# Second cross-attention: scores from the normalized tokens times one product of Wq and K per batch, layer norm's scale and bias on the tokens

## The reference

```python
xn = _layer_norm(_layernorm(x), ln_scale, ln_bias)       # normalized twice, then scale and bias
q = (xn @ Wq).reshape(B, T, 8, 64).transpose(0, 2, 1, 3) * 64 ** -0.5      # Wq: 256 x 512
k, v = jnp.split(y @ Wkv, 2, axis=-1)                    # y: the context, 77 rows a batch; 8 heads of 64
sim = jnp.einsum('bhid,bhjd->bhij', q, k)                # 1024 x 77 a head
attn = softmax(sim)
out = jnp.einsum('bhij,bhjd->bhid', attn, v) @ Wo
x = x + tanh(g_xattn[1]) * out
```

## Time and profile before

| | |
|---|---|
| device time, median of 3 runs | 1934.1 us (1932.99 to 1936.02) |
| the profiled execution | 1928.68 us, its span 1926.9 us |
| granted TensorE clock over the span | 0.987 |
| TensorE busy over the span | 1822.4 us (95%) |
| VectorE, ScalarE, GpSimd busy | 1169.6, 1066.1, 732.6 us |
| second cross-attention | about 917 to 1142 us |

### The profile page before, as it was taken

One profiled execution on the slowest core, in us unless ns is written; L12 is line 12 of the kernel. 1 busy time (PEld: TensorE's weight loads), 2 busy tenths in 40 slices (PEclk: granted clock), 3 DMA queues, 4 the chain that ended last, 5 costly groups with the idle time before them and its releaser, 6 DMA issues.

```text
span 1926.9 us, 59938 instructions
## 1 busy us (share of the span) xinstructions
PE 1822.4 (95%) x26285; PEld 1488.6 (77%) x26285; DVE 1169.6 (61%) x1646; ACT 1066.1 (55%) x1883; POOL 732.6 (38%) x1008
## 2 busy tenths in 40 slices
PE   6999799999999999999899988999999999999996
PEld 4666578888877888888799877888788777888775
DVE  7888533332423333232555549888888888888785
ACT  5666444443434344343344546777677677777663
POOL 6999500000010000000233333564656565655542
PEclk9999999999999999999899999999999999999999
DMA  5332100000000000010211024212432142224210
GB/s 163 106 112 70 50 1 22 1 23 1 22 7 17 22 1 23 0 68 6 75 41 46 24 93 106 75 56 61 118 85 65 56 124 81 63 62 119 58 53 31
DMA packets 147003, 106.21 MB, mean 55 GB/s; under 512 B 19992, under 2 KB 143152, under 8 KB 146736
## 3 DMA queue, kind: packets, MB, share of 16 engines
q1 hardware_dynamic: 146736, 102.28, 18.0%
HBM read 76.77 MB, written 25.49 MB: 53 GB/s over the span
## 4 chain that ended last, share of the span: by engine, by line
PE 40%; ACT 6%; issue 3%; DVE 2%; POOL 0%; DMA 0%; POOLq 0%; DVEq 0%; ACTq 0%
PE E_ps_o L2009 12%; PE E_ps_s L1990 5%; PE E_ps_o L1954 5%; PE C_ps_y L1086 3%; PE E_ps_o L1971 3%; PE C_ps_m L1047 2%; PE E_ps_o L1961 2%; PE C_ps_s L1062 2%; ACT head L2197 2%; ACT e_raw L2208 1%; ACT E_prob L2171 1%; PE C_ps_t L1073 1%; DVE E_negmax L2487 1%; ACT e_raw L2254 1%; PE E_ps_o L2030 1%
## 5 line engine op out<-in xcount | busy, mean ns | idle before, releaser
L2171 ACT ACTIVATE E_prob<-E_ps_s,E_negmax 128x1024 f32<-128x1024 f32 x256 | 284.9, 1116 | 145.2 <-DVE E_negmax L2487 144.8
L2487 DVE TENSOR_REDUCE E_negmax<-E_ps_s 128x1 f32<-128x1024 f32 x256 | 301.5, 1220 | 87.6 <-PE E_ps_s L1990 87.3
L2494 DVE STREAM_TRANSPOSE E_prob<-E_prob 128x1024 f32<-128x1024 f32 x256 | 303.9, 1225 | 23.9 <-ACT E_prob L2171 11.4
L2009 PEld LDWEIGHTS E_ps_o<-E_prob,E_vrep 32*64 32x64 f32 x15872 | 232.3, 130 | 71.2 <-ACT head L2197 55.8
L2009 PE MATMUL E_ps_o<-E_prob,E_vrep 32*64 32x128 f32 x15872 | 265.0, 274 | 17.9 <-issue 8.4
L1588 ACT ACTIVATE F_raw<-F_ps,ffn_scales 128x512 f32<-128x512 f32 x128 | 88.4, 690 | 287.9 <-PE F_ps L1490 287.9
L1490 PE MATMUL F_ps<-F_ha,ffn_w_rounded 128*128 128x512 f32 x1024 | 240.7, 396 | 0.0
L1490 PE MATMUL F_ps<-F_hb,ffn_w_rounded 128*128 128x512 f32 x1024 | 240.2, 395 | 0.0
L1490 PEld LDWEIGHTS F_ps<-F_ha,ffn_w_rounded 128*128 128x128 f32 x1024 | 191.2, 188 | 48.1 <-issue 1.7
L1490 PEld LDWEIGHTS F_ps<-F_hb,ffn_w_rounded 128*128 128x128 f32 x1024 | 192.4, 188 | 46.5
L2390 POOL TENSOR_TENSOR head<-head 128x512 f32<-128x512 f32 x93 | 119.2, 1281 | 256.3 <-ACT head L2197 256.3
(11 more groups left out here) (306 smaller groups left out, 3761.8 us busy)
## 6 DMA issues: line engine op xcount, KB each, us to landing
E_vrep<-E_v_all SPq DMA_DIRECT2D x128, 256.0 KB, 3.1
shared<-in_L_ffn_h_wT SPq DMA_DIRECT2D x16, 512.0 KB, 3.9
E_v_all<-E_vst SPq DMA_DIRECT2D x32, 256.0 KB, 2.2
C_x<-x SPq DMA_DIRECT2D x20, 256.0 KB, 4.2
F_x<-x SPq DMA_DIRECT2D x9, 512.0 KB, 3.8
A_x<-in_x SPq DMA_DIRECT2D x16, 256.0 KB, 5.1
x<-A_x SPq DMA_DIRECT2D x16, 256.0 KB, 2.2
x<-F_x SPq DMA_DIRECT2D x16, 256.0 KB, 2.1
```

What stands on the lines that cost most here:

```text
L2009: mm = pe.matmul(low[64 * j:64 * j + 64, g, :], vrep[rows, slot, KB // 4 * (quarter % 2) + k, dh * j:dh * (j + 1)], prob[rows, u % 2, :, j ...
L2171: act.activation(prob[:, s // UT % 2, s % UT, j, :], ps_s[:, j, :], ACT.Exp, bias=negmax[:, at:at + 1], scale=1.0, accum_out=den[:, 2 * c ...
L2487: dve.tensor_reduce(negmax[:, at:at + 1], ps_s[:, j, :], AX.X, ALU.max, negate=True).then_inc(d_max, 1)
L2494: dve.transpose(at, at).then_inc(d_t, 1)
```

## The change

The q projection goes. Once per batch, K of every head is multiplied by the transposed Wq of that head (`qk_proj`, two chunks k of the model dimension), which gives a matrix `qk` of 256 x 616, kept as hi and lo fp32r tiles: ScalarE writes hi with the softmax scale, VectorE lo. The scores of a tile are the transposed tokens (stationary, hi and lo) times `qk` (moving, 308 columns for 4 heads). Norm's scale and bias are put on the tokens when they leave PSUM: ScalarE's copy becomes two activations with scale and bias, VectorE's `x_low` first computes the same in fp32 (`xf`) and then subtracts. `qbias`, `wq_hi`, `wq_lo`, `q` and the 16 one-column instructions go. K's and V's projections stand in one step (8b - 7), `qk_proj` in the next two (8b - 6, 8b - 5), `u_proj` in two groups (four blocks, one block) at 8b - 4 and 8b - 3; `ps_u` has two banks for one, `ps_m` one for two. Wq is laid out transposed on the way in.

```diff
-        K_AT, V_AT, U_AT = {-7: 0}, {-6: 0}, {-2: (0, 0), -1: (0, 1), 0: (0, 2)}
+        KV_AT, M_AT, U_AT = {-7: 0}, {-6: (0, 0), -5: (0, 1)}, {-2: (0, 0), -1: (0, 1)}
...
-            K_AT[8 * b - 7], V_AT[8 * b - 6] = b, b
-            U_AT.update({8 * b - 5 + i: (b, i) for i in range(3)})
-        U_BLOCKS = ((0, 1), (2, 3), (4,))
+            KV_AT[8 * b - 7] = b
+            M_AT.update({8 * b - 6 + i: (b, i) for i in range(2)})
+            U_AT.update({8 * b - 4 + i: (b, i) for i in range(2)})
+        U_BLOCKS = ((0, 1, 2, 3), (4,))
...
+            def kv_proj(b):
...
+                for i, (w, made) in enumerate(((wk, e_k), (wv, e_v))):
+                    for c in range(C):
+                        for k in range(DC):
+                            mm = pe.matmul(ps_u[:, i, c * S:(c + 1) * S], w[:, k, c * P:(c + 1) * P],
+                                           cx[:, b % 2, k, :], start=k == 0, stop=k == DC - 1)
+                    mm.then_inc(made, 1)
+
+            def qk_proj(b, k):
+                pe.wait_ge(k_made, b + 1)
+                pe.wait_ge(v_made, b + 1)
+                if k:
+                    pe.wait_ge(m_out, 2 * b + 1)
                 for c in range(C):
...
+                    for g in range(RG):
+                        rows = slice(RT * g, RT * (g + 1))
+                        mm = pe.matmul(ps_u[:, g, c * S:(c + 1) * S], wqT_sb[rows, c, k * P:(k + 1) * P], kt[rows, c, :],
+                                       start=True, stop=True)
+                mm.then_inc(e_m, 1)
...
-            def q_proj(n):
-
-                pe.wait_ge(x_out_of, n + 1)
...
             def scores(T):
                 n, t = divmod(T, 2)
                 b = n // PB
-                pe.wait_ge(q_made, n + 1)
+                pe.wait_ge(x_out_of, n + 1)
                 if T % (2 * PB) == 0:
-                    pe.wait_ge(k_made, b + 1)
+                    pe.wait_ge(m_out, 2 * b + 2)
                 if T:
                     pe.wait_ge(d_sub, T)
-                for c in range(C):
-                    for g in range(RG):
-                        rows = slice(RT * g, RT * (g + 1))
-                        mm = pe.matmul(ps_s[:, g, c * HR * S:(c + 1) * HR * S], q[rows, n % 2, c, t * TOK:(t + 1) * TOK],
-                                       kt[rows, b % 2, c, :, :], start=True, stop=True)
+                for g in range(G):
+                    ops = [(k, a, m) for k in range(DC) for a, m in split_passes(xt, qk)]
+                    for i, (k, a, m) in enumerate(ops):
+                        mm = pe.matmul(ps_s[:, g, 0:4 * S], a[:, n % 2, k, t * TOK:(t + 1) * TOK],
+                                       m[:, b % 2, k, 4 * S * g:4 * S * (g + 1)], start=i == 0, stop=i == len(ops) - 1)
                 mm.then_inc(e_s, 1)
...
-                act.activation(xt[0][:, n % 2, :, :], ps_m[:, 0, :].rearrange("p (c w) -> p c w", c=DC),
-                               ACT.Copy).then_inc(x_hi, 1)
...
+                for k in range(DC):
+                    ins = act.activation(xt[0][:, n % 2, k, :], ps_m[:, k * PAIR:(k + 1) * PAIR], ACT.Identity,
+                                         bias=ln_sb[:, 1, k:k + 1], scale=ln_sb[:, 0, k:k + 1])
+                ins.then_inc(x_hi, 1)
...
+            def qk_evacuate(b, k):
+                act.wait_ge(e_m, 2 * b + k + 1)
                 if b >= 2:
                     act.wait_ge(e_s, 2 * PB * (b - 1))
...
+                act.activation(qk[0][:, b % 2, k, :].rearrange("p (c g s) -> p g c s", g=RG, s=S),
+                               ps_u[:, :, 0:C * S].rearrange("p g (c s) -> p g c s", s=S),
+                               ACT.Copy, scale=SCALE).then_inc(m_hi, 1)
...
             def x_low(n):
                 dve.wait_ge(x_hi, n + 1)
...
+                for k in range(DC):
+                    own.link(dve.tensor_scalar(xf[:, k, :], ps_m[:, k * PAIR:(k + 1) * PAIR], ln_sb[:, 0, k:k + 1],
+                                               ln_sb[:, 1, k:k + 1], ALU.mult, ALU.add))
+                own.wait()
+                dve.tensor_tensor(xt[1][:, n % 2, :, :], xf[:, :, :], xt[0][:, n % 2, :, :],
+                                  ALU.subtract).then_inc(x_out_of, 1)
+
+            def qk_low(b, k):
+                dve.wait_ge(m_hi, 2 * b + k + 1)
+                for g in range(RG):
+                    hi, lo = (m[:, b % 2, k, :].rearrange("p (c g s) -> p g c s", g=RG, s=S)[:, g, :, :] for m in qk)
+                    ins = dve.scalar_tensor_tensor(out=lo, in0=ps_u[:, g, 0:C * S].rearrange("p (c s) -> p c s", s=S),
+                                                   scalar=SCALE, in1=hi, op0=ALU.mult, op1=ALU.subtract)
+                ins.then_inc(m_out, 1)
```

More of the change, by code:

```diff
@@ L874, in cross_attention @@
     B, _, S = ctxT.shape
-    HD = wqT.shape[1]
+    HD = wkT.shape[1]
     dh = HD // H
@@ L907, in sb @@
             return ctx.enter_context(nc.sbuf_tensor(f"{tag}_{name}", shape, dt))
-        qbias = sb("qbias", [P, C])
-        kt = sb("kt", [P, 2, C, HR, S])
+        kt = sb("kt", [P, C, S])
+        qk = [sb("qk_hi", [P, 2, DC, H * S], F32R), sb("qk_lo", [P, 2, DC, H * S], F32R)]
         vt = sb("vt", [P, (C + 1) * (TWO + P)])
@@ L1033, in x_transpose @@
                         each = head[:, 2 * n + t, :] if n < HEAD else xn[:, n % 2, t, :]
-                        mm = pe.transpose(ps_m[:, 0, at:at + TOK], each[:, c * P:(c + 1) * P], ident[:, :])
+                        mm = pe.transpose(ps_m[:, at:at + TOK], each[:, c * P:(c + 1) * P], ident[:, :])
                 mm.then_inc(e_x, 1)
-            def q_proj(n):
-                pe.wait_ge(x_out_of, n + 1)
[L1040 to L1049, removed]
             def scores(T):
@@ L1090, in _ @@
             x_transpose(0)
[L1091 to L1096, removed]
             for T in STEPS:
@@ L1102, in _ @@
                     p_transpose(T, 0)
[L1103 to L1107, removed]
+                if not odd and 0 < n + 2 < NP:
+                    x_transpose(n + 2)
                 if 0 <= T < TILES:
@@ L1111, in _ @@
                     out(T - 1)
[L1112 to L1115, removed]
+                if T in KV_AT:
+                    kv_proj(KV_AT[T])
+                if T in M_AT:
+                    qk_proj(*M_AT[T])
                 if T in U_AT:
@@ L1184, in _ @@
             act.activation(warm[:, :], warm[:, :], ACT.Exp)
[L1185 to L1188, removed]
             for T in STEPS:
@@ L1192, in _ @@
                     prob_out(T, 0)
-                if 0 <= n + 2 < NP:
-                    if odd:
-                        q_evacuate(n + 2)
-                    elif n + 2:
-                        x_evacuate(n + 2)
+                if not odd and 0 < n + 2 < NP:
+                    x_evacuate(n + 2)
                 if 0 <= T < TILES:
@@ L1340, in _ @@
                     x_low(0)
-                    for k in range(DC):
-                        ins = dve.tensor_scalar(wq[0][:, k, :], wq_raw[:, k, :], ln_sb[:, 0, k:k + 1], None, ALU.mult)
-                    ins.then_inc(wq_hi, 1)
-                    dve.wait_ge(wq_hi, 1)
-                    for k in range(DC):
-                        ins = dve.scalar_tensor_tensor(out=wq[1][:, k, :], in0=wq_raw[:, k, :],
-                                                       scalar=ln_sb[:, 0, k:k + 1], in1=wq[0][:, k, :],
-                                                       op0=ALU.mult, op1=ALU.subtract)
-                    ins.then_inc(wq_lo, 1)
                 b, p = divmod(T + 12, 8)
@@ L2640, in gated_layers @@
         c_ln = ctx.enter_context(nc.sbuf_tensor("c_ln", [P, 2, DC], F32))
-        HD, rows = t["L1_xattn_Wq"].shape[1], "(c p) n -> p c n"
-        c_wq, c_wk, c_wv = (shared[:, i, :].rearrange("p (c n) -> p c n", n=HD) for i in range(3))
-        c_wo = shared[:, 3, :].rearrange("p (c n) -> p c n", n=D)
+        HD, rows = t["L1_xattn_Wk"].shape[1], "(c p) n -> p c n"
+        c_wk, c_wv = (shared[:, i, :].rearrange("p (c n) -> p c n", n=HD) for i in (1, 2))
+        c_wq, c_wo = (shared[:, i, :].rearrange("p (c n) -> p c n", n=D) for i in (0, 3))
         early = ((c_wq, t["L1_xattn_Wq"].rearrange(rows, p=P)),
```

75 lines of the change are left out of this document (32 added, 43 removed).

## The result

The changed kernel took 1914.8 us (median of four runs, 1912.1 to 1917.7), the kernel before 1933.9 beside it: a ratio of 0.990, 95% interval 0.988 to 0.992, 19 us less. Forecast were 12.5 us less and a time of 1915.5 to 1929.0. The profiled execution took 1917.1 us, its span 1914.7: 12.2 us less than the span before.

The account below looks back on a forecast made before the run. TensorE's queue was taken to bound the second cross-attention. Terms -40.3 + 18.5 + 6.3 + 0.5 + 2.2 = -12.8 us, called -12.5, taken off the 1934.1 median gave 1921.6 us; range 1915.5 to 1929.

Parts of the forecast that it names:

- Bound: Second cross-attention, after the first few tiles: the stage lasts as long as TensorE's queue, busy 189.1 of 190 us.
- B: Rival: VectorE's loop takes over in the second cross-attention, giving 11 us back; total -1.5, 1932.6 us; chance 0.09.
- Term (1): TensorE behind the scores of tile 3: pairs 2 to 15 lose their q projection, 14 x 2.88 = -40.3 us.
- Term (2): Scores on TensorE: twelve 308-column fp32r instructions at 143 ns, 1.71 us a tile, +0.66; +18.5 us over 28 tiles.
- C: Rival: 308-column scores matmuls miss the fp32r rate, 260 ns each; total +28, 1962 us, slower than before; chance 0.06.
- Term (3): Wq times K on TensorE: 1.05 us per batch and chunk, three batches behind the split, +6.3 us.
- Term (4): Once per batch VectorE's remainder of chunk 0 delays the residual that TensorE's output needs: +0.5 us, at worst 5.1.
- Term (5): Stage start to the end of scores(3): two serial Wq-K rounds replace qbias and q projection, +2.2 us (0.2 to 5.1).
- x_low becomes ... a 0.68 subtraction: +0.8 us: VectorE, per pair: two tensor_scalar from PSUM (0.41 each) and a 0.68 subtraction, +0.8 us, hidden under TensorE's work.

Follow-up runs that it names:

- dense_start: Changed kernel plus ten unused fp32r matmuls of 512 columns in TensorE's three waits at the stage's start; stage 205.6 us against 204.7.

## Why the prediction was right and wrong

*Bound.* Right: TensorE's queue sets the stage, before and after; VectorE never took over (B), although it came near enough to delay two outputs per batch.

*Term (1), q projection,* -40.3: right. *Term (2), scores:* 1.70 us for 1.71; right, and C is out with it (141 ns where it decides at 181). The rule that the prediction quotes from the Trainium skill ("TensorE: Matmul & The Clock Gate", Back-to-back issue gap) would have given 1.57; the trace does not agree with it here either. *Term (3), products:* 1.05 us as said, but the scores behind each cost 0.2 more, +1.2 for six.

*Missing term.* The transposes behind the scores became 0.15 us shorter, 28 x 0.15 = -4.2 us. The sentence "K and V projections keep their matmuls ... nothing on TensorE" and term (2) priced matmuls alone and never the change of mode between them.

*Term (4), the new wait:* the mechanism (the residual late behind VectorE's queue) was right, the size failed. I had 0.15 us per batch, behind the Wq-K remainder; that one measured 0.24, and a larger one of 0.68 came in another step, +2.7 for three batches where the sum had 0.5. The step that failed is "x_low becomes ... a 0.68 subtraction: +0.8 us": the subtraction takes 1.29 us, because both operands now lie in SBUF beside GpSimd.

*Term (5), the start:* 2.5 us in the first trace for 2.2; 4.8 in those where the clock comes back later.

Small changes that the sum left out, such as 3.53 us for the K and V projections in one step where it had 3.48, add 0.4. By these terms the stage gets -40.3 + 18.2 + 6.3 + 1.2 - 4.2 + 2.7 + 0.4 + 2.5 = -13.2, or -10.9 with the later clock; 13.2 and 10.9 are measured against the 217.9 of before. So the forecast for the stage (-12.8) was right in its large terms, and as close as it was by luck: two misses, -4.2 and +3.4 (1.2 + 2.2), cancelled.

*The number itself* failed in two steps. The first is "I take the gain off the median: 1934.1 - 12.5". It gives the run the gain of the stage alone and rests it on three runs. Outside the stage the runs show a steady 1.0 us in the handover, which the sum put at nothing ("the way out ... is as before" and no word on the way in) and whose cause stays open, and perhaps 0.8 in the last stage. The level of 1934 came back in none of the later comparisons: the kernel before then stood at 1926 to 1928. From 1926 the same forecast would have been 1913.5, against 1910 measured. The second step is the width: I read the three runs of before, 0.2% apart, as what executions of the kernel differ by; 72 runs in later jobs lie between 1916 and 1935 around 1926. A range of -6 to +7 us around the forecast time was too narrow for that. Why the timed runs say 16 to 18 us where the traces of both programs say 12.5 stays open; the granted clocks of the executions that were traced point to chance.

## What to carry to other kernels

Price what stands between two groups of matmuls, not the groups alone: a step that changes the rows in use costs its neighbours, and removing it pays there. When an elementwise step gets an intermediate tile, look where both operands of the next instruction lie and which engine works beside it; from PSUM the same subtraction took half the time. And when the gain is a per cent, take the length of the stage from several traces, and sort them by what the clock did at its start: within one kind it repeated to 0.4 us, where the kinds lie 2.3 to 2.6 apart and whole runs spread over 10. Compare one kind with the same kind.

## What the runs showed of the hardware

A fp32r matmul with 128 weight columns followed another after 120 ns at 256 columns, 141 at 308 and 233.5 at 512: nearly a straight line, which has 143 at 308.

The start of `dense_start` had TensorE busy for 15.6 of the 16 us from 922 to 938, with projections and products of 77 columns and ten dense matmuls of 512, and the granted clock was 0.50 throughout, the level of 1.2 GHz; it came back within scores 0. In the changed kernel it came back at the end of scores 0 or within the u product behind them, and in three of five traces it fell again behind a gap of 2.2 us after scores 1.

A VectorE subtraction of 128x512 with both inputs in SBUF took 1.29 us beside GpSimd and 0.69 with GpSimd idle or with one input in PSUM. Entering and leaving the mode of 64 rows once cost TensorE 0.28 us.

The chain of waits put a wait down to ScalarE's evacuation (ended 994.03) that was for VectorE's residual (994.01): where two engines end together, take the one away. And it shows only work on the chain: of the 0.66 us that it seems to leave idle there, 0.22 were transposes.
